# A decoder layer on one core: the shift of the second normalisation worked out by ScalarE instead of VectorE

## The chip, the cores and the metric

The kernel runs on one core of a Trainium2 chip. The metric is the device time of one execution in microseconds (us). The kernel before was timed in 3 runs; their median is 1630.95 us.

## What is computed

The reference is one decoder layer over x of 8 batches x 512 rows x 512 channels, float32. Each of its three parts reads a layer normalisation of x and adds its result to x:

```python
x = x + self_attention(layernorm(x))                    # dilated, segments of 128 rows, 16 heads of 32
x = x + cross_attention(layernorm(x), ctx, Wq, Wkv, Wout)   # causal over 512 positions, 16 heads
x = x + ffn(layernorm(x), w_gate, w_up, w_down)         # silu(gate) * up, block-quantised operands

def layernorm(x, eps=1e-05):
    m = mean(x); v = var(x)
    return (x - m) / sqrt(v + eps)
```

The change concerns the second of the three normalisations, the one in front of the cross attention. With rstd = 1 / sqrt(v + eps) it is computed as x * rstd + shift, where shift = -m * rstd is one number per row.

## The kernel before, in words

A first block prepares the weights (to about 140 us). After it the engines run lists of instructions that are written out by hand, one list per engine, each in its own fixed order; semaphores alone couple them. A batch has 4 tiles of 128 rows. The program for each batch b has two stages:

- the cross attention of batch b, 16 units of four heads by 128 rows;
- then a stage of 21 steps (i = 0 to 20), in which the feed-forward part of batch b (16 chunks, one per step, i = 0 to 15) is interleaved with the self attention of batch b + 1 and, in steps 16 to 20 (the "head"), with the start of its cross attention: transposing the normalised tiles, and projecting k and q.

Batch 0 has its self attention alone, ahead of everything (146 to 184 us in the profile). The last batch's feed-forward part has no next batch beside it.

In the interleaved stage a tile t of the next batch goes through four steps, 4t + 1 to 4t + 4 (`part_of`): VectorE takes mean and variance of the tile after self attention (`moments_of`, L495, step 4t + 4), GpSimd raises the variance to the power -1/2 (`power`, L503), VectorE forms shift (`shift2_of`, L513) in the next step, and ScalarE writes the normalised tile xn (`normalise2`, L519) two steps later, or, for the last tile, in the same step. So shift is formed in steps 5, 9, 13 and 17, and xn is written in steps 7, 11, 15 and 17. In steps 5 and 9 VectorE rounds the feed-forward part's next input tile behind shift (`round_x`, L830, the fp8 tile q<-x_f); in step 13 the next chunk's product follows (`gated`, L834, L838).

Other names in the rows: `take_xq` (L983) copies the transposed feed-forward input to SBUF on ScalarE, xq_t; `take_inter` (L998) does the same for a chunk of the hidden layer, iq_t; `high_xt2` and `low_xt2` (L922, L751) split the transposed xn into two parts, x_t, on ScalarE and VectorE; `take_k` (L939) copies k. On TensorE L1203 is the down projection, L1181 gate and up, L1192 the transposition of a chunk, L1089 that of xn, and L529 the q, k and v projections. On GpSimd L696 is the multiplication of a tile by block scales, L506 is `power`.

In the rows the program's digits are left out of names: shift is shift2, q is q8, x_t is x_t2, p is p2.

Of the kernel before, what the change touches and what calls it, by code (L numbers as in the profile page):

```python
# [21 lines left out]
ACT = mybir.ActivationFunctionType  # L22
AX_X = mybir.AxisListType.X

P = 128
# [81 lines left out]
def decoder_layer(nc, x, ctx_t, wq_t, wkv_t, wo_t, w_gate, w_up, w_down, out):  # L107
# [3 lines left out]
    T = N // P  # L111
# [15 lines left out]
    with es:  # L127
        def sb(name, shape, dt=F32):
            return es.enter_context(nc.sbuf_tensor(name, shape, dt))

        def sem(name):
            return es.enter_context(nc.semaphore(name))
# [24 lines left out]
        moments = sb("moments", [P, 3 * T, 2])  # L157
        var_eps = sb("var_eps", [P, 3 * T])
        rstd = sb("rstd", [P, 3 * T])
        shift2 = sb("shift2", [P, T])  # L160
        xn1 = sb("xn1", [P, 2, D])
        tmp1 = sb("tmp1", [P, 2, D])
# [46 lines left out]
        def where(label):  # L209
            return SLOT[slot_of[label][0]]  # L210
# [9 lines left out]
        def until_filled(eng, label):  # L220
            s, k = slot_of[label]
            eng.wait_ge(filled[s], k + 1)

        def until_freed(eng, label):
            s, k = slot_of[label]
            eng.wait_ge(freed[s], k + 1)

        def free(ins, label):
            ins.then_inc(freed[slot_of[label][0]], 1)
# [4 lines left out]
            "rstd1_ready", "rstd2_ready", "rstd3_ready",  # L234
            "dve_chain",
            "ctx_high", "ctx_ready",
            "xn1_ready", "x1_ready", "shift2_ready", "xn2_ready",
            "xt2_high",
            
            "nmx_ready", "p2_ready", "values_done", "rx_ready",  # L240
# [3 lines left out]
        S = {name: sem(name) for name in signals}  # L244
# [234 lines left out]
        def part_of(i):  # L479
            return divmod(i - 1, 4)  # L480

        def by_head(ap):
            return ap.rearrange("p (h d) -> p h d", h=H)
# [11 lines left out]
        def moments_of(dve, link, src, p, t):  # L495

            k = (p - 1) * T + t % T
            link(dve.bn_stats(stats[:, k, :], src))  # L498
            link(dve.bn_aggr(moments[:, k, :], stats[:, k, :]))
            dve.tensor_scalar(var_eps[:, k:k + 1], moments[:, k, 1:2], EPS, None,  # L500
                              ALU.add).then_inc(S[f"var{p}_ready"], 1)
# [7 lines left out]
        def normalise(dve, dst, src, p, t):  # L509
            k = (p - 1) * T + t % T  # L510
            return dve.tensor_scalar(dst, src, moments[:, k, 0:1], rstd[:, k:k + 1], ALU.subtract, ALU.mult)  # L511

        def shift2_of(dve, t):  # L513
            k = T + t % T
            dve.wait_ge(S["rstd2_ready"], t + 1)
            dve.scalar_tensor_tensor(out=shift2[:, t % T:t % T + 1], in0=moments[:, k, 0:1], scalar=-1.0,
                                     in1=rstd[:, k:k + 1], op0=ALU.mult, op1=ALU.mult).then_inc(S["shift2_ready"], 1)

        def normalise2(act, t):  # L519
            k = T + t % T  # L520
            act.wait_ge(S["shift2_ready"], t + 1)
            act.activation(xn[:, t % T, :], x_in[:, t % T, :], ACT.Identity, bias=shift2[:, t % T:t % T + 1],
                           scale=rstd[:, k:k + 1]).then_inc(S["xn2_ready"], 1)
# [29 lines left out]
        def attend_vector(dve, link, b, i):  # L553
            t, part = part_of(i)
            g = b * T + t
            if i == 0:
                dve.wait_ge(x_loaded[0], 32 * (b + 1))
                moments_of(dve, link, x_in[:, 0, :], 1, b * T)

                dve.wait_ge(S["ctx_high"], b + 1)  # L560
                dve.tensor_tensor(ctx_hl[:, 1, :], ctx_in[:], ctx_hl[:, 0, :].bitcast(F32),
                                  ALU.subtract).then_inc(S["ctx_ready"], 1)
            if i == 1:
                dve.wait_ge(S["rstd1_ready"], b * T + 1)
                normalise(dve, xn1[:, 0, :], x_in[:, 0, :], 1, b * T).then_inc(S["xn1_ready"], 1)
            if part == 1 and 0 <= t < T - 1:
                dve.wait_ge(x_loaded[(t + 1) // 2], 32 * (b + 1))
                moments_of(dve, link, x_in[:, t + 1, :], 1, g + 1)
            if part == 2 and 0 <= t < T - 1:

                dve.wait_ge(S["rstd1_ready"], g + 2)
                normalise(dve, xn1[:, (t + 1) % 2, :], x_in[:, t + 1, :], 1, g + 1).then_inc(S["xn1_ready"], 1)
            if part == 2 and 0 <= t < T:
                for r in range(2):
                    until_freed(dve, ("scores1", g, r))
                link(dve.tensor_reduce(sum1[:, t % 2, :], e1[:, t % 2].rearrange("p r (c k) -> p c r k", k=HALF),
                                       AX_X, ALU.add))
                link(dve.reciprocal(rcp1[:, t % 2, :], sum1[:, t % 2, :]))
                label = ("out1", g)
                until_filled(dve, label)  # L580
                if g >= 2:
                    dve.wait_ge(S["x1_ready"], g - 1)
                for e in range(2):
                    rows = slice(e * HALF, (e + 1) * HALF)
                    last = dve.tensor_tensor(by_head(tmp1[rows, t % 2, :])[:, e:H:2, :],  # L585
                                             where(label)[rows, 0, 0:D // 2].rearrange("p (h d) -> p h d", d=HD),
                                             rcp1[rows, t % 2, :].unsqueeze(2).to_broadcast([HALF, H // 2, HD]),
                                             ALU.mult)
                free(last, label)
            if part == 3 and 0 <= t < T:  # L590
                dve.wait_ge(S["x1_ready"], g + 1)
                moments_of(dve, link, x_in[:, t, :], 2, g)
            if part == 0 and 1 <= t <= T:

                shift2_of(dve, g - 1)

        def attend_scalar(act, b, i):
            t, part = part_of(i)
# [26 lines left out]
            if part == 2 and 1 <= t < T:  # L625
                normalise2(act, g - 1)
            if part == 0 and t == T:
                normalise2(act, g - 1)
# [40 lines left out]
        with nc.Block() as block:  # L669
# [77 lines left out]
            def _(dve):  # L747
# [119 lines left out]
                for i in range(P1_STEPS):  # L867
                    attend_vector(dve, link, 0, i)
                    head(0, i)
                for b in range(B):  # L870
# [26 lines left out]
                    if not last:  # L897
                        attend_vector(dve, link, b + 1, 0)
                    take_y(b * T + 3)
                    if not last:  # L900
                        attend_vector(dve, link, b + 1, 1)
# [396 lines left out]
```

## Time and profile before

| | us |
|---|---|
| median of 3 runs | 1630.95 (1624.5 to 1632.29) |
| the profiled execution | 1628.43 |
| its span, first to last instruction | 1626.6 |
| TensorE matmuls busy in the span | 1372.0 (84%) |
| VectorE busy | 1152.6 (71%) |
| ScalarE busy | 859.4 (53%) |
| GpSimd busy | 546.8 (34%) |

The busy shares are means over stages with different limits. The rows further below are therefore taken stage by stage: times in them are microseconds from the start of the span, an idle time in square brackets is that of the engine just ahead of the row, with what ended it.

### The profile page before, as it was taken

The page shows a single profiled execution, that of the slowest core. Times are in us where ns is not written, and L with a number is a line of the kernel's source. Part 1 is how long each engine was busy: PE and PEld are TensorE (multiplying, and loading weights), DVE is VectorE, ACT ScalarE, POOL GpSimd, SP SyncE. Part 2 cuts the span into 40 slices and gives each one's busy share as a digit, 9 for nine tenths or more (in the row PEclk, how much of TensorE's full clock was granted, in tenths as well). Part 3 has the DMA queues.
Part 4 walks back from the last instruction along what each step waited for, and adds up shares of the span by engine and source line. Part 5 has one row for each costly group of instructions (what it writes and reads, how often), then busy time and mean ns, then how long its engine had stood idle before and what let it go on. Part 6 is the DMA issues. An engine that isn't in the chain of part 4 may idle for free.

```text
span 1626.6 us, 31184 instructions
## 1 busy us (share of the span) xinstructions
PE 1372.0 (84%) x11267; PEld 792.3 (49%) x11344; DVE 1152.6 (71%) x2475; ACT 859.4 (53%) x2098; POOL 546.8 (34%) x494
## 2 busy tenths in 40 slices
PE   0223999889998899889998999889988899889987
PEld 0112665445544565445544564455544564455533
DVE  8995555885569656985679555985579556975577
ACT  2542564556635664556635564556635664556622
POOL 5883100660037201660047201660047201750055
PEclk9999999999999999999999999999999999999999
DMA  6321000000010000000010000000010000000001
GB/s 199 98 78 39 1 2 14 21 14 15 2 27 15 20 1 15 21 14 14 2 27 14 21 1 17 18 19 9 2 27 14 21 2 27 8 21 2 2 0 26
DMA packets 25285, 36.07 MB, mean 22 GB/s; under 512 B 2480, under 2 KB 10672, under 8 KB 25136
## 3 DMA queue, kind: packets, MB, share of 16 engines
q1 hardware_dynamic: 25136, 34.09, 7.8%
q8 instruction: 93, 1.52, 0.4%
q14 instruction: 56, 0.46, 0.1%
HBM read 25.69 MB, written 8.39 MB: 21 GB/s over the span
## 4 chain that ended last, share of the span: by engine, by line
PE 43%; DVE 32%; ACT 7%; issue 6%; POOL 3%; DMA 0%; SPq 0%; ACTq 0%; POOLq 0%; DVEq 0%
PE psum L1103 9%; PE psum L1120 9%; PE psum L529 8%; DVE top L812 6%; PE psum L1141 5%; DVE inter L838 4%; PE psum L1157 4%; DVE q L808 3%; PE psum L1106 3%; ACT p L957 3%; DVE nmx L762 2%; DVE top L815 2%; DVE stats L498 2%; DVE x_f L511 2%; DVE tmp L585 1%
## 5 line engine op out<-in xcount | busy, mean ns | idle before, releaser
L762 DVE TENSOR_REDUCE nmx<-psum 128x2 f32<-128x1024 f32 (+3 forms) x256 | 210.7, 823 | 167.0 <-PE psum L1106 166.3
L506 POOL TENSOR_TENSOR rstd<-var_eps,minus_half 128x1 f32<-128x1 f32 x96 | 58.2, 610 | 794.2 <-DVE var_eps L500 793.9
L957 ACT ACTIVATE p<-psum,nmx 128x384 f32<-128x384 f32 (+3 forms) x512 | 265.8, 527 | 64.0 <-DVE nmx L762 42.9
L775 DVE COPY pt<-psum 128x512 f32<-128x512 f32 (+3 forms) x256 | 124.7, 487 | 129.1 <-PE psum L1120 127.5
L1120 PE MATMUL psum<-ident,p 128*128 128x128 f32 x1280 | 204.8, 281 | 12.5 <-ACT pt L981 6.9
L1103 PE MATMUL psum<-k_f,q_f 32*128 32x512 f32 (+3 forms) x1024 | 206.9, 480 | 5.8 <-ACT p L957 5.3
L696 POOL TENSOR_TENSOR inter<-inter,rscale 128x512 f32<-128x512 f32 x128 | 140.1, 1095 | 143.7 <-DVE rscale L846 134.1
L1203 PE MATMUL psum<-wd_sb,iq_t 128*128 128x512 bf16 x483 | 135.3, 394 | 35.9 <-DVE x_res L855 29.3
L1120 PEld LDWEIGHTS psum<-ident,p 128*128 128x128 f32 x1280 | 138.6, 140 | 53.4 <-issue 19.0
L981 ACT COPY pt<-psum 128x512 f32<-128x512 f32 (+3 forms) x256 | 109.2, 426 | 97.8 <-PE psum L1120 95.5
L1181 PE MATMUL psum<-wg_sb,xq_t 128*128 128x512 bf16 x504 | 134.7, 391 | 20.3 <-DVE inter L838 20.3
L995 ACT ACTIVATE silu<-psum 128x512 f32<-128x512 f32 x128 | 76.4, 597 | 142.4 <-PE psum L1181 142.2
L696 POOL TENSOR_TENSOR iq<-q,scale 128x512 bf16<-128x512 fp8e4 x128 | 143.7, 1123 | 8.7 <-DVE q L808 8.7
L1003 ACT COPY iq_t<-psum 128x512 bf16<-128x512 bf16 x128 | 74.9, 585 | 123.9 <-PE psum L1192 123.9
L1181 PE MATMUL psum<-wu_sb,xq_t 128*128 128x512 bf16 x510 | 136.2, 391 | 0.1
L1157 PE MATMUL psum<-wo_sb,xn 128*128 128x512 f32 x256 | 118.0, 610 | 6.5 <-DVE xn L790 6.5
L428 PE MATMUL psum<-ident_b,w_q 128*128 128x128 bf16 x192 | 26.3, 309 | 112.7 <-POOL w_q L335 108.7
L1103 PEld LDWEIGHTS psum<-k_f,q_f 32*128 32x128 f32 x1024 | 76.9, 183 | 61.7 <-issue 43.2
L838 DVE TENSOR_TENSOR inter<-psum,silu 128x512 f32<-128x512 f32 x128 | 86.2, 674 | 24.6 <-ACT silu L995 23.9
L957 ACT ACTIVATION_READ_ACCUMULATOR p<-psum,nmx 128x1 f32 x512 | 103.0, 201 | 0.0
L529 PE MATMUL psum<-x_t,wq_hl 128*128 128x512 f32 (+1 forms) x480 | 100.1, 358 | 0.3
L1141 PE MATMUL psum<-pt,v_sb 128*32 128x128 f32 x2560 | 96.4, 277 | 3.2
(104 smaller groups left out, 2372.3 us busy)
## 6 DMA issues: line engine op xcount, KB each, us to landing
x_in<-in_x_dram SPq DMA_DIRECT2D x32, 256.0 KB, 4.0
out_dram<-x_res SPq DMA_DIRECT2D x64, 128.0 KB, 2.4
w_raw<-in_w_gate_dram SPq DMA_DIRECT2D x16, 256.0 KB, 2.8
w_raw<-in_w_up_dram SPq DMA_DIRECT2D x16, 256.0 KB, 3.1
w_raw<-in_w_down_dram SPq DMA_DIRECT2D x16, 256.0 KB, 3.9
ctx_in<-in_ctx_t_dram SPq DMA_DIRECT2D x8, 256.0 KB, 2.8
wq_raw<-in_wq_t_dram SPq DMA_DIRECT2D x1, 1024.0 KB, 8.4
wo_sb<-in_wo_t_dram SPq DMA_DIRECT2D x1, 1024.0 KB, 10.1
```

Of the source, the lines that this page charges most:

```text
L529: last = pe.matmul(dst, w, x, start=(n == 0), stop=(stop and n == len(terms) - 1))
L696: pool.tensor_tensor(dst.rearrange("p (n k) -> p n k", k=BLOCK), src.rearrange("p (n k) -> p n k", k=BLOCK), scales.unsqueeze(2).to_broadc ...
L762: dve.tensor_reduce(nmx2[:, u % UNITS, 2 * pr:2 * pr + 2], where(("scores2", oc, qt, pr))[:, :, 0:(qt + 1) * P], AX_X, ALU.max, negate=Tru ...
L775: free(dve.tensor_copy(pt2[:, hh, 0:m], where(label)[:, 0, 0:m]), label)
L838: free(dve.tensor_tensor(inter[:, r, :], where(label)[:, 1, :], silu[:, i % 2, :], ALU.mult), label)
L957: ins = act.activation(p2[:, (4 * u + hh) % P2_RING, 0:m], where(label)[:, hh % 2, 0:m], ACT.Exp, bias=nmx2[:, u % UNITS, hh:hh + 1], accu ...
L1103: pe.matmul(where(label)[:, j, 0:m], q_f[rows, oc % 2, qt * P:(qt + 1) * P], k_f[rows, oc % 2, 0:m], start=True, stop=False)
L1120: last = pe.transpose(where(label)[:, 0, kt * P:(kt + 1) * P], p2[:, (4 * u + hh) % P2_RING, kt * P:(kt + 1) * P], ident[:])
L1141: last = pe.matmul(where(("outT", oc))[rows, 0, qt * P:(qt + 1) * P], v_sb[:, kt, h * HD:(h + 1) * HD], pt2[:, hh, kt * P:(kt + 1) * P], s ...
L1157: last = pe.matmul(where(label)[:, 0, :], out_n[:, oc, t % T * P:(t % T + 1) * P], wo_sb[:, oc, :], start=(oc == 0), stop=(oc == OC - 1))
L1181: last = pe.matmul(where(label)[:, j, :], xq_t[:, t % 2, c * P:(c + 1) * P], w[:, c, m * CH:(m + 1) * CH], start=(c == 0), stop=(c == C - 1))
L1203: last = pe.matmul(where(label)[:, 0, :], iq_t[:, i % RING, j * P:(j + 1) * P], wd_sb[:, 4 * m + j, :], start=(m == 0 and j == 0), stop=(m ...
```

## The change

VectorE's one-column product is taken out. ScalarE, ahead of each xn, computes less_mean = -m (one column, multiplication by a constant) and then shift = less_mean * rstd (one column, the scale read from a tile), each with a semaphore that ScalarE itself waits for before it goes on. 32 VectorE instructions go, 64 ScalarE instructions come. The wait for rstd moves from VectorE to ScalarE, and from the step of the product to the step of xn.

```diff
-        def shift2_of(dve, t):
-            k = T + t % T
-            dve.wait_ge(S["rstd2_ready"], t + 1)
-            dve.scalar_tensor_tensor(out=shift2[:, t % T:t % T + 1], in0=moments[:, k, 0:1], scalar=-1.0,
-                                     in1=rstd[:, k:k + 1], op0=ALU.mult, op1=ALU.mult).then_inc(S["shift2_ready"], 1)
-
         def normalise2(act, t):
             k = T + t % T
+            act.wait_ge(S["rstd2_ready"], t + 1)
+            act.mul(less_mean[:, t % T:t % T + 1], moments[:, k, 0:1], -1.0).then_inc(S["less_mean_ready"], 1)
+            act.wait_ge(S["less_mean_ready"], t + 1)
+            act.activation(shift2[:, t % T:t % T + 1], less_mean[:, t % T:t % T + 1], ACT.Identity,
+                           scale=rstd[:, k:k + 1]).then_inc(S["shift2_ready"], 1)
             act.wait_ge(S["shift2_ready"], t + 1)
             act.activation(xn[:, t % T, :], x_in[:, t % T, :], ACT.Identity, bias=shift2[:, t % T:t % T + 1],
                            scale=rstd[:, k:k + 1]).then_inc(S["xn2_ready"], 1)
...
-            if part == 0 and 1 <= t <= T:
-
-                shift2_of(dve, g - 1)
```

VectorE in step 5 of a feed-forward stage, before:

```order
L846 RECIPROCAL rscale<-scale 128x16 [waits dve_chain]
L808 TENSOR_SCALAR q<-inter 128x512 [waits scaled_ready]
L516 SCALAR_TENSOR_TENSOR shift<-moments,rstd 128x1 [waits rstd2_ready]
L808 TENSOR_SCALAR q<-x_f 128x512 [waits x_scaled]
L838 TENSOR_TENSOR inter<-psum,silu 128x512 [waits silu_ready]
```

and after (line numbers are 3 lower from here on):

```order
L843 RECIPROCAL rscale<-scale 128x16 [waits dve_chain]
L805 TENSOR_SCALAR q<-inter 128x512 [waits scaled_ready]
L805 TENSOR_SCALAR q<-x_f 128x512 [waits x_scaled]
L835 TENSOR_TENSOR inter<-psum,silu 128x512 [waits silu_ready]
L809 TENSOR_REDUCE top<-inter 128x16 [waits freed_A]
```

The product is gone, and the rounding of x_f follows that of the chunk directly.

ScalarE in the head of the same stage (steps 16 to 18), before:

```order
L1003 COPY iq_t<-psum 128x512 [waits filled_C0]
L522 ACTIVATE xn<-x_in,shift,rstd 128x512 [waits shift2_ready]
L928 CAST x_t<-psum 128x4x128 [waits filled_O,filled_B]
L945 COPY k_f<-psum 128x512 [waits filled_T,filled_B]
L1003 COPY iq_t<-psum 128x512 [waits filled_C0]
L928 CAST x_t<-psum 128x4x128 [waits filled_O,filled_C1]
```

and after:

```order
L1000 COPY iq_t<-psum 128x512 [waits filled_C0]
L517 ACTIVATE less_mean<-moments 128x1 [waits rstd2_ready]
L519 ACTIVATE shift<-less_mean,rstd 128x1 [waits less_mean_ready]
L522 ACTIVATE xn<-x_in,shift,rstd 128x512 [waits shift2_ready]
L925 CAST x_t<-psum 128x4x128 [waits filled_O,filled_B]
L942 COPY k_f<-psum 128x512 [waits filled_T,filled_B]
L1000 COPY iq_t<-psum 128x512 [waits filled_C0]
L925 CAST x_t<-psum 128x4x128 [waits filled_O,filled_C1]
```

Two instructions stand ahead of xn, and with it ahead of everything that ScalarE does later in the head. No load of an activation table is added: both lists have 72.

## Rows read from the trace of the kernel before

**Rows 1.** Busy time by stretch: us, PE, PEld, DVE, ACT, POOL, PE clock, DMA

```profile
290.00:356.00 66.00, 55.50 (x513) 30.26 (x518) 62.01 (x153) 37.07 (x56) 46.75 (x47) 1.00 0.04 9
356.00:371.00 15.00, 12.92 (x76) 8.90 (x78) 7.45 (x16) 6.38 (x11) 4.74 (x5) 0.89 0.23 54
```

**Rows 2.** The removed instruction's line: duration in ns, shortest, median, longest

```profile
L516 DVE SCALAR_TENSOR_TENSOR shift<-moments,rstd x32: 159/997/1001, 161.4 to 1453.5; 128x1 f32<-128x1 f32 x32
```

**Rows 3.** Timeline (start, us taken), step 5 of batch 0: DVE, then POOL

```profile
312.99 0.36 DVE L808 TENSOR_SCALAR q<-inter 128x512 fp8e4<-128x512 f32 x1
313.27 1.00 DVE L516 SCALAR_TENSOR_TENSOR shift<-moments,rstd 128x1 f32<-128x1 f32 x1
314.52 0.68 DVE L838 TENSOR_TENSOR inter<-psum,silu 128x512 f32<-128x512 f32 x1
...
313.15 1.10 POOL L696 TENSOR_TENSOR inter<-inter,rscale 128x512 f32<-128x512 f32 x1 [0.92 <-DVE rscale L846]
```

**Rows 4.** Timeline, the same step of the last batch, which forms no shift: DVE

```profile
1580.82 0.36 DVE L808 TENSOR_SCALAR q<-inter 128x512 fp8e4<-128x512 f32 x1
1581.10 1.27 DVE L808 TENSOR_SCALAR q<-x_f 128x512 fp8e4<-128x512 f32 x1
1582.29 0.68 DVE L838 TENSOR_TENSOR inter<-psum,silu 128x512 f32<-128x512 f32 x1
```

**Rows 5.** Timeline, steps 13 to 15 of batch 0: DVE

```profile
349.47 1.00 DVE L516 SCALAR_TENSOR_TENSOR shift<-moments,rstd 128x1 f32<-128x1 f32 x1
350.39 0.68 DVE L838 TENSOR_TENSOR inter<-psum,silu 128x512 f32<-128x512 f32 x1
...
353.39 0.69 DVE L838 TENSOR_TENSOR inter<-psum,silu 128x512 f32<-128x512 f32 x1 [0.61 <-ACT silu L995]
```

**Rows 6.** Timeline, steps 11 to 14 of batch 0: ACT, then PE

```profile
337.19 0.82 ACT L522 ACTIVATE xn<-x_in,shift,rstd 128x512 f32<-128x512 f32 x1
338.08 0.58 ACT L988 COPY xq_t<-psum 128x512 bf16<-128x512 bf16 x1
...
340.92 1.02 PE L1203 MATMUL psum<-wd_sb,iq_t 128*128 128x512 bf16 x4 [0.28 <-DVE x_res L855]
...
348.29 0.38 PE L1192 MATMUL psum<-ident_b,iq 128*128 128x128 bf16 x4 [0.28 <-POOL iq L696]
```

**Rows 7.** Timeline, the head behind batch 1's feed-forward part, all engines

```profile
545.25 0.55 POOL L506 TENSOR_TENSOR rstd<-var_eps,minus_half 128x1 f32<-128x1 f32 x1 [0.21 <-DVE var_eps L500]
545.83 0.16 DVE L516 SCALAR_TENSOR_TENSOR shift<-moments,rstd 128x1 f32<-128x1 f32 x1 [0.66 <-POOL rstd L506]
...
546.02 0.81 ACT L522 ACTIVATE xn<-x_in,shift,rstd 128x512 f32<-128x512 f32 x1 [0.45 <-DVE shift L516]
...
547.68 0.60 ACT L1003 COPY iq_t<-psum 128x512 bf16<-128x512 bf16 x1
...
548.34 1.04 PE L1203 MATMUL psum<-wd_sb,iq_t 128*128 128x512 bf16 x4 [0.69 <-ACT iq_t L1003]
```

**Rows 8.** Timeline, the head behind batch 0's feed-forward part: ACT

```profile
363.07 0.82 ACT L522 ACTIVATE xn<-x_in,shift,rstd 128x512 f32<-128x512 f32 x1
...
364.84 0.58 ACT L1003 COPY iq_t<-psum 128x512 bf16<-128x512 bf16 x1
```

**Rows 9.** ACT by line and shape (busy us, mean ns); then L522, its waits (us, times)

```profile
L957 ACT ACTIVATE p<-psum,nmx 128x512 f32<-128x512 f32 x128 | 86.6, 683 | 37.8 <-PE psum L1120 21.1 <-DVE nmx L762 16.7
L995 ACT ACTIVATE silu<-psum 128x512 f32<-128x512 f32 x128 | 76.4, 597 | 142.4 <-PE psum L1181 142.2
...
L957 ACT ACTIVATE p<-psum,nmx 128x128 f32<-128x128 f32 x128 | 46.4, 374 | 0.0
...
L522 ACT ACTIVATE xn<-x_in,shift,rstd x32: 813/816/836, 162.9 to 1453.7; 128x512 f32<-128x512 f32 x32
...
  DVE shift L516: 2.4, 6
```

**Rows 10.** Busy time by stretch, the start of batch 0's head (columns as in rows 1)

```profile
358.80:362.20 3.40, 3.40 (x13) 2.24 (x14) 1.49 (x5) 1.17 (x2) 2.98 (x3) 0.50 0.00 0
```

More of the change, by code:

```diff
@@ L159, in decoder_layer @@
         rstd = sb("rstd", [P, 3 * T])
+        less_mean = sb("less_mean", [P, T])
         shift2 = sb("shift2", [P, T])
@@ L236, in decoder_layer @@
             "ctx_high", "ctx_ready",
-            "xn1_ready", "x1_ready", "shift2_ready", "xn2_ready",
+            "xn1_ready", "x1_ready", "less_mean_ready", "shift2_ready", "xn2_ready",
             "xt2_high",
```

## Prediction

> **What bounds the kernel now.** I read the busy times by stretch first, then the timeline of single steps, then the durations by line. The feed-forward stage of a batch is bound by VectorE: it is busy for 62.01 of 66.00 us, while ScalarE is busy for 37.07 [rows 1]. In the head that follows, VectorE is busy for only 7.45 of 15.00 us and TensorE for 12.92 [rows 1]; there the order of the waits decides, not an engine's load. The same instruction is therefore worth something different in each stage. Of the 32 normalisations 4 lie in batch 0's own self attention, 7 x 3 inside a feed-forward stage, and 7 in the heads behind one.
>
> **What the change removes.** VectorE loses 32 products. Their median is 997 ns, against 159 ns for the shortest [rows 2]. In step 5 the reason is visible: the product starts at 313.27 us, GpSimd's multiplication has begun at 313.15 us and ends at 314.25 us, and the product's record ends with it, at 314.27 us [rows 3]. One column does not take 1 us; the instruction stands still until GpSimd is done. So I ask who stands still in its place when it is gone.
>
> - Steps 5 and 9, 14 places. Behind the product comes the rounding of x_f. The last batch runs the same step without a product, and there that rounding takes 1.27 us: it is the one that is held [rows 4]. From the start of the chunk's rounding to the start of L838 it is 314.52 - 312.99 = 1.53 us with the product [rows 3] and 1582.29 - 1580.82 = 1.47 us without [rows 4]. The gain is 0.06 us a place, 14 x 0.06 = 0.84 us, on the engine that bounds the stage.
> - Step 13, 7 places. No rounding of x_f follows, and L838 can start at 349.47 in place of 350.39 us, 0.92 us sooner [rows 5]. But one chunk later VectorE waits 0.61 us for ScalarE's silu, which doesn't depend on this product [rows 5]. That wait grows to 1.53 us. I count 0; what is late next is the silu.
> - Step 17 and batch 0's own self attention, 11 places. VectorE waits for rstd in front of the product (0.66 us in the head of batch 1 [rows 7]) and is spared that wait. What follows it there is off the path: the head goes on through xn. I count 0.
>
> **What the change adds.** Two one-column instructions and two waits of ScalarE for itself. No row shows a one-column ACTIVATE, so I take its fixed part from wider ones. From 512 to 128 columns p falls from 683 to 374 ns, 0.805 ns a column [rows 9]. With that, silu (constants only) leaves 597 - 411 = 186 ns for one column, p (one operand read from a tile) 374 - 102 = 272 ns, and xn (two such operands) 816 - 411 = 405 ns [rows 9]. less_mean is nearest to silu, shift to p. For a wait I take the gap from shift's end to xn's start in the head, 545.99 to 546.02 us, 0.03 us [rows 7]. The pair costs 0.186 + 0.03 + 0.272 + 0.03 = 0.52 us of ScalarE. From below: neither pays for an operand, 2 x 0.186 + 2 x 0.03 = 0.43 us. From above: both cost what xn's fixed part costs, and a wait of an engine for itself costs three times that gap, 2 x 0.405 + 2 x 0.10 = 1.0 us. Could GpSimd hold them up as it does VectorE? xn reads three tiles of the same memory and stays between 813 and 836 ns in all 32 cases [rows 9], so no.
>
> The Trainium skill, page "ScalarE: Activation LUTs", section "What ACT_TABLE_LOAD costs", gives 186 ns + 0.833 ns a column for an ACTIVATE with constants and about 93 ns for each operand read from a tile. By that the pair would be an estimated 0.187 + 0.280 + 0.06 = 0.53 us, and the sum below would rise by less than 0.1 us; the rows' price stands.
>
> Where does the pair lie?
>
> - Steps 7, 11 and 15, 21 places. ScalarE has idle time behind them. The tightest is step 11: xn ends at 338.01 us and xq_t begins at 338.08 us, so 0.07 us are free there [rows 6]. TensorE then has 0.28 us to spare before L1203, which waits for VectorE, and 0.28 us again before L1192 [rows 6]. Together that is 0.63 us, more than 0.52 us. I count 0; if that cover were used up, each of the 7 batches would pay what is over 0.63 us.
> - The heads. Here everything hangs on xn: ScalarE runs from xn through k to iq_t, and TensorE waits 0.69 us for that iq_t [rows 7] before the down projection and the q projection, with which the next cross attention starts. In the head of batch 1 xn starts 0.22 us after rstd is there (545.80 to 546.02 us, [rows 7]). In its place come 0.03 + 0.52 = 0.55 us, so xn is 0.33 us later. xn waits for shift in six places, which are the heads of five batches and batch 0's own [rows 9]: 6 x 0.33 = 1.98 us. Behind batches 0 and 3 ScalarE itself is late, so that the pair counts whole, 0.52 us; but from xn to iq_t these take 364.84 - 363.07 = 1.77 us [rows 8] against 1.66 us [rows 7], because TensorE holds iq_t there, and 0.11 us of it is hidden: 2 x 0.41 = 0.82 us.
>
> **The sum.** +1.98 + 0.82 - 0.84 = +2.0 us. Against the profiled execution that is 1628.43 + 2.0 = 1630.4 us. It lies 2.5 us below the median of the three runs; carried over to that median I predict 1630.95 + 2.0 = 1633.0 us. With the pair at 0.43 us the sum is 6 x 0.24 + 2 x 0.32 - 0.84 = +1.2 us; with the pair at 1.0 us and no gain on VectorE it is 6 x 0.81 + 2 x 0.89 = +6.6 us, and (1.0 - 0.63) x 7 = 2.6 us for step 11 on top, +9.2 us. A difference of 0.5%, 8.2 us, is about what a measurement of this kernel can tell from none; the three runs alone span 7.8 us.
>
> **Rivals.**
>
> - Step 13's time comes back. If the silu comes sooner once the chunk in front of it does, 0.92 us in each of 7 batches are won: 1633.0 - 6.4 = 1626.6 us. For it: VectorE bounds the stage as a whole. Against it: the silu ends a chain on ScalarE, and VectorE waits for it already [rows 5]. Chance 0.08.
> - All stretched products come back whole. Then 21 x 0.92 = 19.3 us go, and the heads keep their 2.8 us: 1630.95 - 16.5 = 1614.5 us, faster. For it: the median of 997 ns [rows 2]. Against it: the last batch, where the next instruction is held instead [rows 4]. Chance 0.04.
> - The pair costs ScalarE 1 us or more, because a wait for its own result is dearer than one for another engine. From 0.63 us on it shows in step 11 too, and at 1.0 us the sum is the +9.2 us of above: 1640.2 us, slower. For it: no row shows ScalarE waiting for itself. Against it: three gaps of 0.1 us would be needed where 0.03 us is seen [rows 7]. Chance 0.08. The Trainium skill, same page, section "Rules for kernel authors", speaks against this change: it sends multiplications to VectorE. It argues from the time per element, and these have one column.
> - TensorE's clock falls in the longer head. Batch 0's head begins with a stretch at a granted 0.50, 1.2 GHz [rows 10]. If a longer wait put that projection (24 matmuls, about 3 us) at half clock in 7 heads, about 7 x 3 = 21 us are lost: 1654 us. Against it: a head is 15 us long [rows 1] and grows by 0.4 us. Chance 0.04.
> - The change doesn't do what it says: the two lists show the product gone, the pair in place, and no added table load. Chance 0.01.
>
> **How the numbers follow.** The forecast, +1.2 to +6.6 us with a median that moves by some 3 us between measurements, has 0.75. The range takes in the first rival below and the third above: 1626 to 1641 us; outside lie about 0.04 + 0.04 + 0.01 and half of the edges. Faster by over 0.5% (below 1622.8 us): the second rival, 0.04, and 0.01 of chance, 0.05. Slower by over 0.5% (above 1639.1 us): about half of the third, the fourth, and 0.01, 0.09. The rest, 0.86, is no change that can be told.
>
> **What would show it.** In the changed profile: q<-x_f of steps 5 and 9 at 1.27 us, as in the last batch; L838 of step 15 waiting for silu some 1.5 us in place of 0.61; less_mean near 0.19 and shift near 0.27 us with gaps of 0.03 us; in the heads xn 0.55 us after rstd, and TensorE's wait for iq_t near 1 us. The prediction is wrong if VectorE's stage gets shorter by over 0.5 us a batch, if the pair takes over 0.63 us, or if the head grows by over 1 us.

## The result, and the profile after

The changed kernel takes 1634.56 us (median of 11 runs, 1632.47 to 1638.43). The kernel before, timed beside it, takes 1628.83 us (11 runs, 1624.44 to 1632.29). The ratio is 1.0042, with a 95% interval of 1.0029 to 1.0055: slower, by some 0.4%. The time lies in the predicted range. The forecast was +2.0 us, the medians differ by 5.7 us, so a part of the sum was mis-sized. (The 1630.95 us from which the forecast started was a median of 3 runs; 11 give 2.1 us less.)

The profiled execution took 1633.83 us. The first lines of its page, with the span and the busy time of each engine:

```profile
span 1632.0 us, 31216 instructions
...
PE 1370.7 (84%) x11267; PEld 793.1 (49%) x11344; DVE 1144.3 (70%) x2443; ACT 875.2 (54%) x2162; POOL 547.1 (34%) x494
```

VectorE lost 8.3 us of busy time against the kernel before and ScalarE gained 15.8 us, yet the span grew by 5.4 us. As before, the averages don't say where. The two new lines, durations in ns (shortest, median, longest):

```profile
L517 ACT ACTIVATE less_mean<-moments x32: 204/207/228, 159.6 to 1455.4; 128x1 f32<-128x1 f32 x32
```

```profile
L519 ACT ACTIVATE shift<-less_mean,rstd x32: 295/297/299, 159.8 to 1455.7; 128x1 f32<-128x1 f32 x32
```

207 and 297 ns against estimates of 186 and 272 ns: 21 and 25 ns dearer. **Where nothing waits for them** they are free. Step 5 of batch 0 goes as the last batch's did before [rows 4]. VectorE's timeline (start, us taken):

```profile
309.89 0.36 DVE L805 TENSOR_SCALAR q<-inter 128x512 fp8e4<-128x512 f32 x1
...
310.17 1.26 DVE L805 TENSOR_SCALAR q<-x_f 128x512 fp8e4<-128x512 f32 x1
...
311.36 0.68 DVE L835 TENSOR_TENSOR inter<-psum,silu 128x512 f32<-128x512 f32 x1
```

x_f's rounding is now the one that is held, and from the chunk's rounding to L835 (L838 before) it is 311.36 - 309.89 = 1.47 us, against 1.53 us with the product [rows 3]. In step 15 VectorE's wait for silu has grown from 0.61 us [rows 5] to 1.13 us:

```profile
350.16 0.69 DVE L835 TENSOR_TENSOR inter<-psum,silu 128x512 f32<-128x512 f32 x1 [1.13 <-ACT silu L992]
```

**The heads** are where the time is lost. I measure a head from the last L835 (L838) of a feed-forward part to the first L759 (L762), with which the next cross attention's softmax begins. Behind batch 2 it was 735.53 - 718.11 = 17.42 us; VectorE's timeline of the kernel before:

```profile
718.11 0.69 DVE L838 TENSOR_TENSOR inter<-psum,silu 128x512 f32<-128x512 f32 x1 [0.62 <-ACT silu L995]
...
735.53 2.50 DVE L762 TENSOR_REDUCE nmx<-psum 128x2 f32<-128x1024 f32 x2 [3.92 <-PE psum L1106]
```

It is now 734.37 - 715.16 = 19.21 us:

```profile
715.16 0.69 DVE L835 TENSOR_TENSOR inter<-psum,silu 128x512 f32<-128x512 f32 x1 [1.13 <-ACT silu L992]
...
734.37 2.50 DVE L759 TENSOR_REDUCE nmx<-psum 128x2 f32<-128x1024 f32 x2 [3.90 <-PE psum L1103]
```

The pair alone is not 1.79 us long. ScalarE's timeline of this head, after:

```profile
724.61 0.59 ACT L1000 COPY iq_t<-psum 128x512 bf16<-128x512 bf16 x1 [1.55 <-PE psum L1189]
725.09 0.21 ACT L517 ACTIVATE less_mean<-moments 128x1 f32<-128x1 f32 x1
725.33 0.30 ACT L519 ACTIVATE shift<-less_mean,rstd 128x1 f32<-128x1 f32 x1
725.66 0.82 ACT L522 ACTIVATE xn<-x_in,shift,rstd 128x512 f32<-128x512 f32 x1
```

From less_mean to xn it is 725.66 - 725.09 = 0.57 us (0.52 us estimated). But xn starts 10.50 us after L835, against 726.93 - 718.11 = 8.82 us before, that is 1.68 us later. The rest stands ahead of the pair: ScalarE is still copying iq_t, having waited 1.55 us for TensorE. GpSimd's rstd, for which less_mean should have been waiting, is there at 723.22 + 0.55 = 723.77 us, 1.32 us before less_mean starts:

```profile
723.22 0.55 POOL L507 TENSOR_TENSOR rstd<-var_eps,minus_half 128x1 f32<-128x1 f32 x1 [0.20 <-DVE var_eps L501]
```

TensorE's timeline of the same place, first before, then after:

```profile
721.30 1.48 PE L1203 MATMUL psum<-wd_sb,iq_t 128*128 128x512 bf16 x3 [2.27 <-DVE x_res L855]
722.58 0.63 PE L1192 MATMUL psum<-ident_b,iq 128*128 128x128 bf16 x4
723.41 1.37 PE L1089 MATMUL psum<-ident,xn 128*128 128x128 f32 x8 [0.20 <-DVE tmp L585]
724.61 1.03 PE L1203 MATMUL psum<-wd_sb,iq_t 128*128 128x512 bf16 x4
```

```profile
720.47 1.97 PE L1086 MATMUL psum<-ident,xn 128*128 128x128 f32 x8 [1.08 <-DVE tmp L585]
722.23 1.91 PE L1200 MATMUL psum<-wd_sb,iq_t 128*128 128x512 bf16 x4
723.93 0.63 PE L1189 MATMUL psum<-ident_b,iq 128*128 128x128 bf16 x4
```

The same down projection takes 1.91 us in place of 1.03. The busy times by stretch tell why (us, PE, PEld, DVE, ACT, POOL, granted clock, DMA). Before:

```profile
720.70:723.90 3.20, 2.40 (x10) 1.44 (x12) 3.00 (x7) 0.58 (x1) 2.16 (x3) 0.50 0.39 85
724.10:727.00 2.90, 2.90 (x22) 2.05 (x21) 1.26 (x5) 1.73 (x4) 2.39 (x3) 1.00 0.01 3
```

After:

```profile
719.00:722.00 3.00, 1.92 (x11) 1.65 (x10) 1.76 (x5) 0.97 (x2) 2.32 (x3) 0.50 0.40 86
722.00:725.60 3.60, 3.60 (x16) 2.40 (x15) 2.32 (x5) 1.75 (x5) 1.56 (x3) 0.50 0.00 0
```

In both kernels TensorE stands still in this head, waiting for VectorE's x_res and tmp, and in both a stretch at 1.2 GHz follows. In the kernel before it runs from 2.5 us behind L838 and is over when the second down projection begins. After, it begins 3.7 us behind L835 and reaches over the transpositions of xn and the second down projection to some 10.5 us: 3.60 of 3.60 us of work at half speed, with the head's chain behind it. It is not only later but longer: 6.8 us in place of 3.4 us. In the four heads of before that take 17.42 or 17.43 us the stretch lies somewhere between 2.5 and 6.4 us behind L838 and is 3.4 us long. After the change it lies between 3.5 and 10.7 us and is 6.8 us long in four heads, and between 5.1 and 8.8 us and 3.4 us long in the other three.

Summed over the two profiled executions, one of each kernel: the seven heads +8.7 us; VectorE's steps 4 to 12 in these seven batches -0.65 us; the last batch +1.9 us in steps 0 to 4, -0.4 us in steps 4 to 8 and +1.3 us at its end; the attention stages -2.3 us (two stretches at 1.2 GHz in the output projection before, which this execution lacks); and the part up to the first cross attention -3.2 us. That last part changes from 185.4 to 191.0 us between all the profiles of this study. Most of that is made in the first 20 us, in the block that prepares the weights and that the change doesn't touch: VectorE's first w_pow comes within 0.2 us of a multiplication on GpSimd, and takes 3.5 us when GpSimd is first, 0.9 us when VectorE is. VectorE's timeline, before and after:

```profile
12.35 3.51 DVE L379 TENSOR_SCALAR w_pow<-w_y 128x1536 int32<-128x1536 int32 x1 [0.37 <-POOL w_y L328]
```

```profile
11.57 0.90 DVE L380 TENSOR_SCALAR w_pow<-w_y 128x1536 int32<-128x1536 int32 x1
```

Of the twelve profiles, before, e1, e4, e5, e7 and e9 have the long one, the others the short one. It is taken as spread here; how often each kernel falls into either order no run shows. The sum is 8.7 - 0.65 + 2.8 - 2.3 - 3.2 = +5.35 us, beside the span's +5.4 us.

### The profile page after: what moved, and what is told of

Same layout as the page of the kernel before. It is cut to its first block, busy times and chain, and to the rows that moved or that the text cites. A ratio compares the mean times of both kernels' runs of the same rounds, so it can differ in the third digit from the quotient of the medians.

```text
span 1632.0 us, 31216 instructions
## 1 busy us (share of the span) xinstructions
PE 1370.7 (84%) x11267; PEld 793.1 (49%) x11344; DVE 1144.3 (70%) x2443; ACT 875.2 (54%) x2162; POOL 547.1 (34%) x494
## 4 chain that ended last, share of the span: by engine, by line
PE 44%; DVE 31%; ACT 7%; issue 6%; POOL 3%; DMA 0%; SPq 0%; ACTq 0%; POOLq 0%; DVEq 0%
PE psum L1100 9%; PE psum L1117 9%; PE psum L529 8%; DVE top L809 6%; PE psum L1138 4%; DVE q L805 4%; DVE inter L835 4%; PE psum L1154 4%; PE psum L1103 3%; ACT p L954 3%; DVE nmx L759 3%; DVE top L812 2%; DVE stats L499 2%; PE psum L1200 2%; DVE x_f L512 2%
## 5 line engine op out<-in xcount | busy, mean ns | idle before, releaser
L759 DVE TENSOR_REDUCE nmx<-psum 128x2 f32<-128x1024 f32 (+3 forms) x256 | 210.7, 823 | 167.5 <-PE psum L1103 166.8
L1178 PE MATMUL psum<-wg_sb,xq_t 128*128 128x512 bf16 x504 | 130.8, 381 | 23.6 <-DVE inter L835 20.9
L1178 PE MATMUL psum<-wu_sb,xq_t 128*128 128x512 bf16 x510 | 132.9, 383 | 0.1
L1154 PE MATMUL psum<-wo_sb,xn 128*128 128x512 f32 x256 | 114.7, 596 | 6.5 <-DVE xn L787 6.5
L835 DVE TENSOR_TENSOR inter<-psum,silu 128x512 f32<-128x512 f32 x128 | 86.2, 674 | 28.6 <-ACT silu L992 28.0
```

Source lines behind the costliest of these rows:

```text
L759: dve.tensor_reduce(nmx2[:, u % UNITS, 2 * pr:2 * pr + 2], where(("scores2", oc, qt, pr))[:, :, 0:(qt + 1) * P], AX_X, ALU.max, negate=Tru ...
L835: free(dve.tensor_tensor(inter[:, r, :], where(label)[:, 1, :], silu[:, i % 2, :], ALU.mult), label)
L1154: last = pe.matmul(where(label)[:, 0, :], out_n[:, oc, t % T * P:(t % T + 1) * P], wo_sb[:, oc, :], start=(oc == 0), stop=(oc == OC - 1))
L1178: last = pe.matmul(where(label)[:, j, :], xq_t[:, t % 2, c * P:(c + 1) * P], w[:, c, m * CH:(m + 1) * CH], start=(c == 0), stop=(c == C - 1))
```

## The experiments

**Theory.** The pair costs about 0.37 us a head, as forecast, and the rest is a stretch at 1.2 GHz that the change moves from TensorE's wait onto its work. **Rivals:** the pair costs more than its own length, directly; or the other 24 places (steps 7, 11, 15), counted at nothing, lose time.

Each ratio below is to the kernel before, run in the same set: 1628.12 us (29 runs) beside e1 to e4, 1626.40 us (21 runs) beside e5 to e8, 1626.89 us (11 runs) beside e9 and e10. The heads of the runs that bear on this, in us, behind batches 0 to 6 (first L759 less last L835, as above):

```
before  18.37 17.65 17.42 18.61 17.41 17.43 17.42
after   19.10 18.73 19.21 18.69 19.21 18.83 19.27
e1      19.07 17.41 17.42 17.42 17.42 17.42 17.41
e2      17.79 17.79 18.83 19.24 18.76 19.16 18.71
e3      17.43 17.64 17.43 17.42 17.44 17.44 17.43
e4      17.77 17.78 17.80 17.80 17.80 17.79 17.79
e7      18.01 to 18.03 in all seven
e9      18.73 18.35 18.36 19.14 19.50 18.10 18.99
e10     17.64 17.42 17.42 17.42 17.42 17.43 17.42
```

**e1, heads on VectorE.** The last tile's shift goes back to VectorE, the other 24 stay on ScalarE:

```diff
+            if part == 0 and t == T:
+                shift2_of(dve, g - 1)
...
         def normalise2(act, t):
+            if t % T == T - 1:
+                act.wait_ge(S["dve_shift"], t // T + 1)
+            else:
```

> The change in 24 of its 32 places; in the last tile of each batch (batch 0's own self attention and the 7 heads) VectorE forms shift as before. Theory (the loss is made in the heads: ScalarE's pair on the path there, and through it the stretches at 1.2 GHz fall later, on TensorE's work): about 1627.9 us, the 1628.8 us of before less 0.9 us of VectorE's time in steps 5 and 9. Rival (the pair in steps 7, 11 and 15 holds something up): about 1634 us, as after the whole change.

Measured: 1627.29 us (12 runs), ratio 1.0001 [0.9986, 1.0016]. The loss is gone, so it is made where the last tile's pair stands; the 24 other places cost nothing that can be measured. In its profile steps 4 to 12 keep their 1.0 us of gain. Its first head takes 19.07 us without the pair: a stretch at 1.2 GHz lies there from 3.2 to 10.0 us behind the feed-forward part's last product (L835 above).

**e2, heads on ScalarE.** The opposite: the pair in the last tile of each batch only, 8 places, the product in the other 24 (condition `t % T < T - 1`, and `1 <= t < T` on VectorE).

> The other part alone: ScalarE's pair in the last tile of each batch only (8 places), VectorE's product in the other 24. Theory (the loss is made in the heads): 1634 to 1636 us, with heads of about 19 us from L838 of step 15 to the first L762 (before 17.4 to 18.6). Rival (the loss is made in steps 7, 11, 15): about 1629 us.

Measured: 1637.7 us (5 runs), ratio 1.0065 [1.0049, 1.0082], above the expected 1634 to 1636 us. The last tile's pair alone brings the loss. In the profile the heads are 6.0 us longer than before and the end of the last batch is 4.0 us longer, at 1.2 GHz from 1618.1 us on. The first two heads show 17.79 us, with the stretch over by 6.5 us behind the feed-forward part's last product, and the third 18.83 us, with the stretch from 5.4 to 8.8 us: in this one execution the same pair is seen without and with the stretch on the work.

**e3 and e4, TensorE kept busy.** To take the stretch away, TensorE gets matmuls of no use in the gap: 9 behind step 15 and 5 ahead of the transposition in step 16, with the helper that the kernel already uses elsewhere (`keep_busy`: a 128x512 product into a PSUM bank that is still free). e3 has them in the kernel before, e4 in the changed one.

```diff
                 def head(b, i):
+                    if i == 4 * T and b:
+                        keep_busy(("k", b * OC), 5)
...
+                        if i == CHUNKS and b + 1 < B:
+                            keep_busy(("k", (b + 1) * OC), 9)
```

> The kernel before, with 9 matmuls of no use on TensorE in the gap behind step 15 and 5 more ahead of the transposition of xn in step 16, into a bank that nobody reads then, so that TensorE stands still for less time ahead of the head. Theory (the granted clock falls to 1.2 GHz because of that gap, and the halved stretch costs the head up to 1.2 us): no halved stretch in the heads, every head 17.4 us or less; 1624 to 1626 us. Rival (the halved stretch lies beside waits and costs nothing): 1628.8 us or more, the added matmuls being in the way.

> The same matmuls of no use in the changed kernel. Theory (of the loss of 5.7 us about 2 us are the pair on the path less VectorE's gain, the rest the halved stretch that falls on TensorE's work): heads of 17.8 us in place of 19.0, 1625 to 1628 us, that is 1 to 2.5 us above the same matmuls in the kernel before. Rival (the pair itself costs the whole loss): about 5.7 us above the same matmuls in the kernel before.

Measured: e3 1622.25 us (12 runs), ratio 0.9967 [0.9954, 0.9979], with e6 the fastest of the study and below the 1624 to 1626 us of the theory. e4 1629.87 us (11 runs), ratio 1.0021 [1.0008, 1.0033]. In e3 the gap behind batch 2 is filled and the clock stays up; TensorE's timeline, then the stretch:

```profile
712.13 2.12 PE L1060 MATMUL psum<-wd_sb,ident_b 128*128 128x512 bf16 x9
714.08 1.03 PE L1203 MATMUL psum<-wd_sb,iq_t 128*128 128x512 bf16 x4
714.94 0.39 PE L1192 MATMUL psum<-ident_b,iq 128*128 128x128 bf16 x4
715.17 1.24 PE L1060 MATMUL psum<-wd_sb,ident_b 128*128 128x512 bf16 x5
716.44 1.09 PE L1089 MATMUL psum<-ident,xn 128*128 128x128 f32 x8
717.37 1.03 PE L1203 MATMUL psum<-wd_sb,iq_t 128*128 128x512 bf16 x4
```

```profile
711.10:714.50 3.40, 3.32 (x43) 1.93 (x42) 3.23 (x7) 1.68 (x4) 2.37 (x3) 1.00 0.00 0
```

With the clock undisturbed in both, a head costs 17.79 us with the pair and 17.42 us without: **the pair is worth 0.37 us a head**, against 0.33 and 0.41 us in the forecast. ScalarE's timeline of e4 shows it by itself, behind rstd as forecast:

```profile
724.36 0.20 ACT L517 ACTIVATE less_mean<-moments 128x1 f32<-128x1 f32 x1 [0.53 <-POOL rstd L507]
724.60 0.29 ACT L519 ACTIVATE shift<-less_mean,rstd 128x1 f32<-128x1 f32 x1
724.93 0.81 ACT L522 ACTIVATE xn<-x_in,shift,rstd 128x512 f32<-128x512 f32 x1
```

But the times speak against the theory: e4 is 7.6 us above e3, where the theory had 1 to 2.5 us and the rival 5.7 us. The stretches are gone from the heads, and the loss in time is not. The profiles differ by 11.0 us: 2.3 us in the heads, 2.8 us in the last batch (next experiment), 4.1 us in the part ahead of the first cross attention (w_pow takes 3.51 us in e4, 0.92 us in e3), 2.4 us in the attention stages (1.7 us of it a stretch at 1.2 GHz), less 0.7 us on VectorE. How much of the 7.6 us the first 20 us of the program make is open.

Nor is e3's gain all the heads'. Its profile is 9.7 us shorter than that of before: 2.1 us in the heads, 4.5 us ahead of the first cross attention, 3.1 us in the attention stages, where the two stretches of before don't occur.

**e5 and e8, the last batch.** In its step 1 VectorE stands still for 0.18 us ahead of x_f's normalisation, where the page names no wait. VectorE and then GpSimd, after:

```profile
1564.68 0.25 DVE L843 RECIPROCAL rscale<-scale 128x16 f32<-128x16 f32 x1
1565.12 1.23 DVE L512 TENSOR_SCALAR x_f<-x_res,moments,rstd 128x512 f32<-128x512 f32 x1 [0.18 <-issue]
```

```profile
1565.01 1.05 POOL L693 TENSOR_TENSOR inter<-inter,rscale 128x512 f32<-128x512 f32 x1 [5.98 <-DVE rscale L843]
```

Before, VectorE was first (1562.27 against 1562.43 us) and it was GpSimd that was held a little:

```profile
1562.27 0.46 DVE L511 TENSOR_SCALAR x_f<-x_res,moments,rstd 128x512 f32<-128x512 f32 x1
```

```profile
1562.43 1.20 POOL L696 TENSOR_TENSOR inter<-inter,rscale 128x512 f32<-128x512 f32 x1 [5.98 <-DVE rscale L846]
```

x_f is on the path here: 1.23 in place of 0.46 us, TensorE's next wait grows from 1.74 to 2.77 us, and its clock falls behind that (granted 0.50 in the 3.3 us that follow, 1.00 at the same place before). The change takes 32 instructions out of VectorE's list, so everything behind lies elsewhere in that list. e5 is e4 with 32 one-column memsets at the start of VectorE's second list, e8 the same without the matmuls of no use:

```diff
                 link = chain(dve, S["dve_chain"])
 
+                for n in range(32):
+                    dve.memset(filler[:, n:n + 1], 0.0)
```

> The changed kernel with the matmuls of no use, and 32 one-column memsets on VectorE at the start of the block after the weights, where it waits for x anyway: as many instructions as the change took out of VectorE's list, so that in the last batch the list is as long up to each instruction as in the kernel before. Theory (in step 1 of the last batch VectorE's instruction stream stands still for about 0.2 us at a place that moves with the length of the list; GpSimd then gets to the shared memory port first, x_f takes 1.23 us in place of 0.46, and the clock falls behind it: 2.8 us in all): steps 0 to 4 of the last batch back from 15.2 to 13.3 us, in all about 1627 us. Rival (the last batch's loss comes from elsewhere): 15.2 us and about 1630 us, as without the memsets.

> The changed kernel with the 32 memsets alone, without the matmuls. Theory: steps 0 to 4 of the last batch back at 13.3 us; the heads stay at about 19 us; 1631.8 us, 2.8 us below the changed kernel's 1634.6. Rival: 1634.6 us.

In both profiles x_f takes 0.46 us again and steps 0 to 4 of the last batch are back from 15.2 to 13.29 us. After, e4 and e7, whose VectorE lists are the same, all have the gap of 0.18 us and x_f at 1.22 or 1.23 us; the other nine profiles have neither at this place. So the place of an instruction in the list decides on the gap, and the gap on who goes first. The +1.3 us at the batch's end don't come with the gap: they are gone in e5 and not in e8, and e9 and e10 have them with x_f at 0.46 us. The times don't follow: e5 1629.99 us (9 runs), ratio 1.0018 [1.0004, 1.0032], no better than e4 (1.0021); e8 1637.21 us (5 runs), ratio 1.0065 [1.0051, 1.0078], if anything worse than the changed kernel (1.0042 [1.0029, 1.0055]), where 1631.8 us were expected. Its heads take 18.7 to 19.3 us, as expected. In e8's profile the last batch wins 1.5 us in steps 0 to 8 and loses 1.7 us at its end, which runs at 1.2 GHz:

```profile
1620.80:1632.80 12.00, 6.52 (x20) 2.32 (x20) 0.69 (x1) 1.23 (x3) 1.15 (x2) 0.50 0.14 30
```

What the gap is worth in time stays open.

**e6, both repairs.** e1 with e3's matmuls: VectorE's gain without the pair in the heads.

> A version that should beat both: the matmuls of no use, shift on VectorE in the last tile of each batch, on ScalarE in the other 24 places. Theory: heads of 17.4 us and 0.06 us less in each of steps 5 and 9: about 1621.4 us, 0.9 us below the kernel before with the same matmuls (1622.25). Rival (the 24 places on ScalarE cost something that the clock hid): 1622.3 us or more.

Measured: 1623.02 us (12 runs), ratio 0.9979 [0.9968, 0.999]. It beats both kernels but not e3; against e3 (measured beside another set of runs) the 0.9 us of gain can't be seen. e5, measured in the same set, is 7.0 us above e6, with its last batch repaired and no stretch in the heads. In the profiles the heads make 2.4 us of it and the part ahead of the first cross attention 5.1 us (w_pow 3.56 and 0.96 us). As with e4 and e3, what the pair costs in time beyond its 0.37 us a head is not explained.

**e7, a third instruction.** e4 with one more one-column instruction and its wait in the heads, to price the chain by itself:

```diff
+            if t % T == T - 1:
+                act.mul(again[:], moments[:, k, 0:1], -1.0).then_inc(S["again_ready"], 1)
+                act.wait_ge(S["again_ready"], t // T + 1)
```

> The changed kernel with the matmuls of no use, and in the last tile of each batch a third one-column instruction ahead of the pair (the same multiplication, into a tile that nobody reads). Theory (every one-column instruction in front of xn is on the head's path): heads of 17.79 + 0.24 = 18.03 us. Rival (the head has slack): 17.8 us.

Measured: heads of 18.01 to 18.03 us, 0.23 us more than e4 (1632.81 us in its one run). ScalarE's timeline:

```profile
725.09 0.20 ACT L519 ACTIVATE again<-moments 128x1 f32<-128x1 f32 x1 [0.53 <-POOL rstd L508]
725.33 0.20 ACT L521 ACTIVATE less_mean<-moments 128x1 f32<-128x1 f32 x1
725.56 0.30 ACT L523 ACTIVATE shift<-less_mean,rstd 128x1 f32<-128x1 f32 x1
725.89 0.81 ACT L526 ACTIVATE xn<-x_in,shift,rstd 128x512 f32<-128x512 f32 x1
```

Each step of the chain costs its own length and a gap of 0.03 to 0.04 us, so ScalarE's wait for its own result is no dearer than the one for VectorE. The rival that priced it at 0.1 us falls.

**e9 and e10, a longer batch with the product back.** If the pair draws the stretch onto the work, e1 is free of it; if it is a matter of when a head comes, any lengthening of the batch will do. e9 is e1 with one matmul of the output projection per batch done twice; e10 is the same with the matmuls of no use in the heads.

```diff
+                        if oc == 0 and t % T == 2:
+                            pe.matmul(where(label)[:, 0, :], out_n[:, oc, t % T * P:(t % T + 1) * P],
+                                      wo_sb[:, oc, :], start=True, stop=True)
```

> Shift on VectorE in the last tile of each batch (the kernel of e1, 1627.3 us), and one matmul doubled in the output projection of each batch, far from the head and on TensorE's path there: every batch is 0.44 us longer, about what the pair adds to a head. Theory (where the 1.2 GHz stretch falls hangs on the length of a batch as a whole: any lengthening of this size makes it wander into the head's work): most heads at 18.4 us or more in place of 17.4, and about 1627.3 + 3.5 + 5 = 1636 us. Rival (the pair, standing in the head, pulls the stretch there): heads stay at 17.4 us, about 1627.3 + 3.5 = 1631 us.

> The same doubled matmul in the kernel with the matmuls of no use (e6, 1623.0 us), where no stretch at 1.2 GHz falls into a head. Both theories: heads of 17.4 us, and 8 x 0.44 = 3.5 us more, about 1626.5 us. It gives the price of the doubled matmul without the clock.

e9: 1641.06 us (6 runs), ratio 1.0088 [1.0067, 1.0108]. The extra matmul takes 0.86 us a batch, about twice what I had expected: the trace has two matmuls for each one added. All seven heads are 18.1 to 19.5 us long although the pair is not in them, and the clock row of the head behind batch 2 reads 0.50 over 3.30 us of work:

```profile
727.60:730.90 3.30, 3.30 (x13) 2.12 (x13) 1.40 (x5) 1.17 (x2) 2.92 (x3) 0.50 0.01 2
```

So the pair in the head isn't needed to make the stretch fall on the work; time added 77 us ahead of the head does it too. e10: 1637.06 us (6 runs), ratio 1.0064 [1.0048, 1.008]. The heads stay at 17.42 us, as expected, but it is 14 us above e6 where 3.5 us were expected. 8 x 0.86 = 6.9 us are the matmul; in every other batch, four in all against one in e6, some 1.7 us are lost to a stretch at 1.2 GHz in the attention stage, which the matmuls in the heads don't cover:

```profile
264.00:290.00 26.00, 24.22 (x116) 11.21 (x114) 13.99 (x34) 6.29 (x15) 5.10 (x6) 0.93 0.14 41
```

e6 had 1.00 at the place of the first:

```profile
264.00:290.00 26.00, 23.55 (x151) 11.67 (x152) 16.49 (x43) 8.60 (x19) 6.60 (x8) 1.00 0.15 41
```

## Why the prediction was right in its range and short in its sum

- **The range.** The forecast started from 1630.95 us, 2.1 us above what 11 runs of the kernel before give, and in the profile the heads' +8.7 us and the last batch's +2.8 us were offset by 5.5 us elsewhere, none of which was forecast. That 1634.56 us comes so near the forecast 1633.0 us is in part luck. By its own signs the prediction failed in one: it called itself wrong if the head grew by over 1 us, and five of the seven did, by 1.1 to 1.9 us. TensorE's wait for iq_t, forecast near 1 us, is 0.24 us behind batch 2 and 0.73 us in e4.
- **Steps 5 and 9, 14 x 0.06 = 0.84 us: right.** 12 of the 14 places gain 0.05 to 0.11 us in the profile; two don't (0.01 us, and 0.17 us the other way), so that the sum there is 0.65 us. In e1 all 14 gain, 0.96 us in sum. The product's 997 ns [rows 2] were never its own: x_f's rounding waits in its place.
- **Step 13 at 0: right.** L835 comes sooner, and the wait for silu in step 15 grows from 0.61 to 1.13 us; from step 13 to step 15 it is 6.23 us in both. The growth is smaller than the 0.92 us named, since an instruction between them is now held in the product's place.
- **The pair, 0.52 us: 0.57 us measured.** All bounds hold. The nearest rows of wider shapes gave 186 and 272 ns, the instructions take 207 and 297 ns, and the gaps are the 0.03 us read off [rows 7].
- **The cover in steps 7, 11 and 15: right.** e1 has the pair there and is at 1.0001.
- **The heads, "6 x 0.33 + 2 x 0.41 = 2.80 us": the step that failed.** The pair itself costs 0.37 us a head, 2.6 us in seven (e4 less e3), so the term was right for what it counted. What it left out is that the clock in the head is not a constant. I had read one row of TensorE at 1.2 GHz, at the start of batch 0's head [rows 10], and taken it for that head's. The other heads have such a stretch too; in the clean ones of before it lay on TensorE's wait for x_res, where it cost nothing, and only behind batches 0 and 3 (18.37 and 18.61 us, the two heads that the sum priced apart) on work. With the change it lies on the transpositions and the down projection in all seven, in four of them twice as long, and costs a further 0.9 to 1.5 us a head: the seven heads of after are 133.0 us in sum, against 7 x 17.79 = 124.5 us undisturbed, 8.5 us; before it was 124.3 against 7 x 17.42 = 121.9 us, 2.4 us. The difference, 6.1 us, and the pair's 2.6 us make the 8.7 us by which the heads grew in the profile. Whether it is the 6.1 us that make the medians differ by 5.7 us is not shown: with the stretches gone from the heads of both kernels (e3, e4) they differ by 7.6 us.
- **The clock rival** had the engine and the head right, and the work, the price and the chance wrong: 21 us for the q projection, at 0.04. The q projection still runs at full clock (3.46 us, 3.48 before); what falls into the stretch is what comes ahead of it, 3.6 us of work that takes up to twice as long but partly beside other waits.
- **The last batch** was in no term: +1.9 us, -0.4 us and +1.3 us in the profile. The first two go with a gap of 0.18 us in VectorE's list; that is shown as a mechanism (e5 and e8 undo it), not as a time. Where the +1.3 us at the end come from is open.
- The other two rivals on the fast side fell: no product came back whole, and step 13's time did not.

Settled are which of the 32 places bring the loss (e1, e2), the price of the pair in a head (e4, e7), that the rest of the heads' growth goes when TensorE's gap is filled (e3, e4), and that heads grow without the pair when the batch gets longer (e9). Not settled is the time as a whole: without stretches in the heads the kernels with the pair are still 7.6 and 7.0 us slower than those without it (e4 and e3, e5 and e6), and the pair itself makes 2.6 us of that. Open too is why the stretch comes back at the same place of each head. In the clean heads of before and e1 one batch follows the next at about 181.0 us, after the change at 182.3 to 182.8 us; that the period decides was argued from e9, not tried in steps.

## What to carry to other kernels

A one-column instruction moved off the bound engine is worth only what its successor doesn't take over, and it costs its whole length where it enters a serial piece between stages (0.23 us a head in e7): price it there first. When such a piece has a gap on TensorE, read the granted clock of every repetition, not of one: a stretch at 1.2 GHz that lies on a wait is free here, and a batch longer by 0.86 us (e9) put it on work. Filling the gap took 2.1 us off the heads in e3's profile, more than the 1.0 us that the moved product saved at best (e1). And when a repair restores the piece that it aims at and the total doesn't follow, as in e4, e5 and e8, the account of the total isn't finished.

## What was not expected of the hardware

- The same head in one execution (e2) costs 17.79 us or 18.7 to 19.2 us: the former with a stretch at 1.2 GHz of 3.4 us that is over by 6.5 us behind the feed-forward part's last product, the latter with one of 3.4 us from 5.1 to 8.8 us or one of 6.8 us from 3.6 to 10.6 us. 0.86 us of work added elsewhere in the batch is enough to change it (e1's heads of 17.4 us, but for the first, become 18.1 to 19.5 us in e9).
- Of VectorE and GpSimd, starting within 0.2 us of each other, whoever is first runs through and the other is held: VectorE first 0.46 us with GpSimd at 1.20 us, GpSimd first 1.05 us with VectorE at 1.23 us (x_f); and in the first 20 us of the program VectorE's w_pow 0.90 or 3.51 us. A gap of 0.18 us without a named releaser turned the order round, and 32 instructions more or fewer in the list ahead move that gap.
